# DLRM tower: the last group's squares added on VectorE, group 2's transposed features copied in three parts from another bank, feature transposes ahead of the embedding

## What is computed

```python
e = stack([tbl_f[ids[:, f]] for f in range(26)])               # 512 x 26 x 64
x = layer_norm(dense @ Wd.T)                                   # 512 x 128
y = layer_norm(e @ Ws.T)                                       # 512 x 26 x 128
y = layer_norm(y mixed over the 26 fields by Wsi)              # 32 projections per channel
T = concat([x, y.T])                                           # 33 x 128 per sample
Z = T @ T.T; Zflat = lower triangle of Z                       # 528 pairs
z = layer_norm(Zflat @ Wl.T)[:, :384]                          # over 512 features
h = relu(concat([z, dense]) @ W_top1 + b_top1)                 # 512
h = relu(h @ W_top2 + b_top2)                                  # 256
out = h @ W_top3
```

## Time and profile before

| | |
|---|---|
| median of 3 runs | 171.63 us (170.33 to 172.66) |
| the profiled execution | 171.68 us |
| its span, first to last instruction | 169.9 us |
| instructions in it | 3523 |
| busy, share of the span | PE 149.0 us (88%), DVE 124.9 (74%), POOL 100.6 (59%), ACT 83.7 (49%) |
| mean granted TensorE clock | 0.97 of full speed |

### The profile page before, as it was taken

One profiled execution on the slowest core, in us unless ns is written; L12 is line 12 of the kernel. 1 busy time (PEld: TensorE's weight loads), 2 busy tenths in 40 slices (PEclk: granted clock), 3 DMA queues, 4 the chain that ended last, 5 costly groups with the idle time before them and its releaser, 6 DMA issues.

```text
span 169.9 us, 3523 instructions
## 1 busy us (share of the span) xinstructions
PE 149.0 (88%) x1382; PEld 107.1 (63%) x1382; DVE 124.9 (74%) x256; ACT 83.7 (49%) x224; POOL 100.6 (59%) x109
## 2 busy tenths in 40 slices
PE   0489878997968797999999899999998999899995
PEld 0324466945545665646978475678876665689994
DVE  6595838978808796777589998486998987993153
ACT  3012243329677829686646465653538363653250
POOL 1777777777777777777777777777777400030000
PEclk9999999579997899999999999999999999999999
DMA  4913651625121111111111111121111100000000
GB/s 104 335 24 58 207 137 41 203 42 147 23 35 25 32 24 23 35 23 34 24 23 34 24 23 35 23 32 28 23 33 27 23 0 4 0 0 4 4 0 0
DMA packets 5728, 8.14 MB, mean 48 GB/s; under 512 B 2357, under 2 KB 3279, under 8 KB 5712
## 3 DMA queue, kind: packets, MB, share of 16 engines
q0 software_dynamic: 3328, 3.41, 10.9%
q1 hardware_dynamic: 1664, 3.65, 6.8%
q10 hardware_dynamic: 720, 0.85, 1.5%
HBM read 7.91 MB, written 0.00 MB: 47 GB/s over the span
## 4 chain that ended last, share of the span: by engine, by line
PE 50%; DVE 17%; ACT 12%; POOL 11%; issue 7%; DMA 1%; DVEq 0%
POOL G L332 11%; PE ps_tail L1116 8%; PE ps_y L1067 6%; PE ps_tail L1132 5%; PE ps_z L1074 5%; PE ps_gq L1042 5%; PE ps_ut L1054 4%; DVE V L794 4%; DVE V L778 3%; PE ps_z L1162 3%; PE ps_tail L1026 3%; ACT sq L438 2%; DVE var L750 2%; DVE var L785 2%; ACT gt L424 2%
## 5 line engine op out<-in xcount | busy, mean ns | idle before, releaser
L332 POOL DMA_INDIRECT G<-in_table_dram,idx x104 | 98.4, 947 | 34.9 <-issue 31.1
L1054 PE MATMUL ps_ut<-S,G 128*128 128x192 f32 (+4 forms) x128 | 21.8, 316 | 0.4 <-DVE G L764 0.4
L778 DVE TENSOR_TENSOR V<-ps_y,bias_y 128x512 f32<-128x512 f32 x32 | 20.5, 682 | 1.5 <-PE ps_y L1067 1.4
L1074 PEld LDWEIGHTS ps_z<-V 128*64 128x64 f32 x448 | 15.1, 142 | 10.0 <-DVE V L794 6.2
L1054 PEld LDWEIGHTS ps_ut<-S,G 128*128 128x128 f32 x128 | 20.1, 199 | 2.0 <-DVE G L764 1.8
L1042 PE MATMUL ps_gq<-gram,gt 128*128 128x128 f32 x104 | 15.9, 293 | 6.0 <-ACT gt L424 5.7
L785 DVE TENSOR_REDUCE var<-sq 128x32 f32<-128x1024 f32 x14 | 17.1, 1220 | 5.4 <-ACT sq L438 5.4
L438 ACT ACTIVATE sq<-V 128x1024 f32<-128x1024 f32 x14 | 14.9, 1061 | 11.1 <-DVE V L778 11.1
L1067 PE MATMUL ps_y<-ut,wcg 64*128 64x512 f32 x64 | 19.5, 686 | 0.5 <-issue 0.4
L1042 PEld LDWEIGHTS ps_gq<-gram,gt 128*128 128x128 f32 x104 | 13.5, 199 | 7.5 <-ACT gt L424 6.5
L1074 PE MATMUL ps_z<-V 128*64 128x67 f32 x448 | 17.1, 231 | 0.2
(11 more groups left out here) (179 smaller groups left out, 235.3 us busy)
## 6 DMA issues: line engine op xcount, KB each, us to landing
G<-in_table_dram,idx POOLq DMA_INDIRECT x104, 2.4
w1z<-in_w_z_dram SPq DMA_DIRECT2D x1, 768.0 KB, 4.3
wl<-in_wl_blocks_dram SPq DMA_DIRECT2D x1, 768.0 KB, 5.8
dns<-in_dense_t_dram ACTq DMA_DIRECT2D x1, 512.0 KB, 4.7
w1d<-in_w_d_dram SPq DMA_DIRECT2D x1, 512.0 KB, 5.1
wl<-in_wl_blocks_dram SPq DMA_DIRECT2D x1, 512.0 KB, 3.7
w2s<-in_w_dram SPq DMA_DIRECT2D x1, 512.0 KB, 3.6
wrow<-in_wsi_rows_dram SPq DMA_DIRECT2D x1, 208.0 KB
```

What stands on the lines that cost most here:

```text
L332: pool.indirect_dma_start(G[:, n // NC, j, g, :], None, table, bass.IndirectOffsetOnAxis(ap=idx[:, k:k + 1], axis=0)).then_inc(gathered[n ...
L778: dve.tensor_tensor(chunk_v(n)[:, g * CB // 2:(g + 1) * CB // 2, :, :], ps_y[:, g, :].rearrange("p (b l q) -> p b l q", l=2, q=NPROJ), bia ...
L1054: mm = pe.matmul(ps_ut[:, chunk % 2, col:col + width], G[:, gp, j, :, :].rearrange("p g d -> p (g d)"), S[:, j, :, :].rearrange("p s q -> ...
L1074: mm = pe.matmul(z_bank(n)[64 * ct:64 * ct + 64, w, s * SLOTS:(s + 1) * SLOTS], V[:, v, 3:SLOTS], V[:, v, :], start=True, stop=True)
```

## The change

It has four parts. In slots 7 and 11, TensorE's `transpose_features` stands ahead of `embed`, and ScalarE's `f_scale` ahead of `ut_copy`. For group 2, the transposes go to the bank `ps_gq`, ScalarE copies them to `zn` in three pieces of 128 columns, and `layer1` waits for one piece at a time in its first block. In the last group, VectorE adds the squares of blocks 3, 0 and 1 into `f_acc` in two additions, and TensorE sums `f_acc` and the square of block 2 by two matmuls instead of four. And GpSimd multiplies the second half of the dense part by `sd3`, in place of VectorE.

```diff
--- before.py
+++ after.py
@@ -160,6 +160,7 @@
         f_scaled = sb("f_scaled", [P, LLIVE, P])
         f_sq = sb("f_sq", [P, LC, GRAN])
         f_sum = sb("f_sum", [P, 1])
+        f_acc = sb("f_acc", [P, GRAN])
         sd3 = sb("sd3", [P, GRAN])
         r3 = sb("r3", [P, GRAN])
         dense_sd = sb("dense_sd", [P, OC1, GRAN])
@@ -220,7 +221,7 @@
             sem("h1_ps"), sem("h1_pre_ready"), sem("h1_ready"), sem("h2_ps"), sem("h2_ready"))
         own_sq_ready, b2_ready, h1_last_ps, h1_scaled, h1_last_pre, h1_last_ready, h2_last_ps, h2_last_ready = [sem(n) for n in (
             "own_sq_ready", "b2_ready", "h1_last_ps", "h1_scaled", "h1_last_pre", "h1_last_ready", "h2_last_ps", "h2_last_ready")]
-        floor2_ready = sem("floor2_ready")
+        floor2_ready, f_acc_ready, dense_sd_pool = sem("floor2_ready"), sem("f_acc_ready"), sem("dense_sd_pool")
         yo_ps, yo_ready, stored = sem("yo_ps"), sem("yo_ready"), sem("stored")
 
         dense_banks = (ps_tail[:, :], ps_z[:, 1, :])
@@ -338,6 +339,11 @@
             pool.tensor_tensor(chunk_v(n), chunk_v(n), r2_pool[:, :].rearrange("p (b l) -> p b l", l=2).unsqueeze(3).broadcast_to([P, CB, 2, NPROJ]),
                                ALU.mult).then_inc(v_pool_ready, 1)
 
+            gp = NG - 1
+            pool.wait_ge(sd3_ready, gp + 1)
+            pool.tensor_tensor(dense_sd[:, half_ocs(1), :], h1_dense[:, half_ocs(1), gp * GRAN:(gp + 1) * GRAN],
+                               sd3[:, :].unsqueeze(1).broadcast_to([P, OC1 // 2, GRAN]), ALU.mult).then_inc(dense_sd_pool, 1)
+
         @block.scalar
         def _(act):
             act.dma_start(wc[:, :], ws_t).then_inc(ld_wc, 16)
@@ -476,7 +482,12 @@
 
             def zn_copy(gp):
                 act.wait_ge(ft_ps, gp + 1)
-                act.copy(zn[:, :, :], tail[:, 0:LLIVE, :]).then_inc(zn_ready, 1)
+                act.copy(zn[:, :, :], tail[:, 0:LLIVE, :]).then_inc(zn_ready, LLIVE)
+
+            def zn_copy_parts(gp):
+                act.wait_ge(ft_ps, gp + 1)
+                for k in range(LLIVE):
+                    act.copy(zn[:, k, :], ps_gq[:, k * P:(k + 1) * P]).then_inc(zn_ready, 1)
 
             def relu1(gp):
                 act.wait_ge(h1_pre_ready, gp + 1)
@@ -539,13 +550,13 @@
                 gt_copy(n)
                 if c < 3:
                     deviation2(n - 2)
+                if c == 3 and gp > 0:
+                    f_scale(gp - 1)
                 ut_copy(n - 1)
                 if c == 0 and gp > 1:
                     relu1(gp - 2)
                 if c == 2 and gp > 0:
                     z_copy(gp - 1)
-                if c == 3 and gp > 0:
-                    f_scale(gp - 1)
                 if n == 3:
                     prepare_means(0)
                 if n == 4:
@@ -608,7 +619,7 @@
             deviation3(gp - 1)
             ut_copy(n)
             f_scale(gp - 1)
-            zn_copy(gp - 1)
+            zn_copy_parts(gp - 1)
             deviation2(n - 1)
             last_square2(n, 0)
             last_square2(n, 1)
@@ -860,16 +871,23 @@
             def last_f_copy(gp):
 
                 for lc in range(LLIVE):
+                    if lc == LLIVE - 1:
+
+                        dve.wait_ge(f_sq_ready, gp + 2)
+                        dve.tensor_tensor(f_acc[:, :], f_sq[:, LLIVE, :], f_sq[:, 0, :], ALU.add).then_inc(f_acc_ready, 1)
                     dve.wait_ge(f_ps, gp + 2 + lc)
                     dve.tensor_copy(f_sb[:, lc, :], last_f_banks[lc]).then_inc(f_ready, 1)
+                dve.wait_ge(f_sq_ready, gp + 3)
+                dve.wait_ge(f_acc_ready, 1)
+                dve.tensor_tensor(f_acc[:, :], f_acc[:, :], f_sq[:, 1, :], ALU.add).then_inc(f_acc_ready, 1)
 
             def last_add_dense(gp):
 
                 dve.wait_ge(sd3_ready, gp + 1)
+                dve.tensor_tensor(dense_sd[:, half_ocs(0), :], h1_dense[:, half_ocs(0), gp * GRAN:(gp + 1) * GRAN],
+                                  sd3[:, :].unsqueeze(1).broadcast_to([P, OC1 // 2, GRAN]), ALU.mult).then_inc(h1_scaled, 1)
                 for h in range(2):
-                    dve.tensor_tensor(dense_sd[:, half_ocs(h), :], h1_dense[:, half_ocs(h), gp * GRAN:(gp + 1) * GRAN],
-                                      sd3[:, :].unsqueeze(1).broadcast_to([P, OC1 // 2, GRAN]), ALU.mult).then_inc(h1_scaled, 1)
-                    dve.wait_ge(h1_scaled, h + 1)
+                    dve.wait_ge((h1_scaled, dense_sd_pool)[h], 1)
                     dve.wait_ge(h1_last_ps, 1 + h)
                     dve.tensor_tensor(h1_pre_last[:, half_ocs(h), :], last_h1_ps[:, h, :, :], dense_sd[:, half_ocs(h), :],
                                       ALU.add).then_inc(h1_last_pre, 1)
@@ -1126,9 +1144,10 @@
 
             def layer1(gp, ocs=range(OC1)):
                 pe.wait_ge(w1_ready, 1)
-                pe.wait_ge(zn_ready, gp + 1)
                 for oc in ocs:
                     for k in range(LLIVE):
+                        if oc == 0:
+                            pe.wait_ge(zn_ready, gp * LLIVE + k + 1)
                         mm = pe.matmul(tail[:, oc, :], w1z[:, k, oc * P:(oc + 1) * P], zn[:, k, :],
                                        start=(k == 0), stop=(k == LLIVE - 1))
                 if OC1 - 1 in ocs:
@@ -1184,13 +1203,12 @@
                                    start=(k == 0), stop=(k == KB - 1))
                 mm.then_inc(f_ps, 1)
 
-            def last_sum_squares(gp, lc):
-
-                place = LAST_ORDER.index(lc)
-                pe.wait_ge(f_sq_ready, gp + 1 + place)
-                mm = pe.matmul(last_ss_ps, ones[:, :], f_sq[:, lc, :], start=(place == 0), stop=(place == LC - 1))
-                if place == LC - 1:
-                    mm.then_inc(ss_ps, 1)
+            def last_sum_squares(gp):
+
+                pe.wait_ge(f_acc_ready, 2)
+                pe.matmul(last_ss_ps, ones[:, :], f_acc[:, :], start=True, stop=False)
+                pe.wait_ge(f_sq_ready, gp + LC)
+                pe.matmul(last_ss_ps, ones[:, :], f_sq[:, LLIVE - 1, :], start=False, stop=True).then_inc(ss_ps, 1)
 
             def last_layer1(gp, ocs):
                 for oc in ocs:
@@ -1231,9 +1249,9 @@
                 gram_rows(n)
                 if c == 2 and gp > 0:
                     spread_pairs(gp - 1)
-                embed(n - 1)
                 if c == 3 and gp > 0:
                     transpose_features(gp - 1)
+                embed(n - 1)
                 pair_products(n - 2)
                 if c == 0 and gp > 1:
                     layer2(gp - 2)
@@ -1287,7 +1305,11 @@
             project_fields(n)
             pair_products(n - 2)
             embed(n)
-            transpose_features(gp - 1)
+            pe.wait_ge(f_ready, gp)
+            pe.wait_ge(q_used, NCHUNK)
+            for k in range(LLIVE):
+                mm = pe.transpose(ps_gq[:, k * P:(k + 1) * P], f_scaled[:, k, :], eye[:, :])
+            mm.then_inc(ft_ps, 1)
             layer1(gp - 1)
             pair_products(n - 1)
             last_pair_products(n, 0)
@@ -1296,15 +1318,10 @@
             spread_pairs(gp)
             layer2(gp - 1, range(1, OC2))
 
-            last_project_pairs(gp, 3)
-            last_project_pairs(gp, 0)
-            last_sum_squares(gp, 3)
-            last_project_pairs(gp, 1)
-            last_sum_squares(gp, 0)
-            last_project_pairs(gp, 2)
-            last_sum_squares(gp, 1)
+            for lc in LAST_ORDER:
+                last_project_pairs(gp, lc)
             last_layer1(gp, range(0, 1))
-            last_sum_squares(gp, 2)
+            last_sum_squares(gp)
             last_layer1(gp, range(1, OC1))
             layer3(gp - 1)
             last_layer2(gp)
```

## The result

The changed kernel takes 173.69 us (median of 6 runs, 172.47 to 174.47) against 171.68 us for the kernel before (6 runs, 170.33 to 172.66) in the same measurement. The ratio is 1.0111 with a 95% interval of 1.0071 to 1.0150: slower by 1.9 us by the ratio and by 2.0 between the medians, and outside the range, which was predicted to end at 172.4.

What follows compares the result with a forecast made beforehand. TensorE was taken to bound the kernel, with 50% of the chain that ended last; the four parts' terms, 0 + 0 - 0.5 + 0, took 171.68 to 171.2 us, range 170.1 to 172.4.

Steps and rivals of the forecast that it cites:

- rival of a mutual lock (B): Last group's dense product: VectorE's and GpSimd's halves exclude each other, the first ReLU comes late, up to 172.3; chance 0.07.
- signs that the prediction listed: Two sums of squares; PE idle about 0.25 in group 2; slots 7, 11 unchanged; GpSimd's dense product 0.5 to 0.7.
- Rival C: Last group's copy, addition and square outlast layer 1's first quarter, or moved embedding's cover fails: 0.1 to 0.3 lost; chance 0.12.
- The cover of VectorE's additions: Slots 7 and 11: embedding halves ready 0.09 and 0.20 before VectorE's additions want them; otherwise late by at most 0.48.
- rival A: Group 2: pair products do not wait for V, so the earlier layer 1 gains 0.27 more, 170.9; chance 0.08.

## Why the prediction was wrong

The forecast of 171.2 us, half a microsecond faster, missed one part, which is worth more than the three others together. For these three its sum, 0.5, is close to the 0.6 of the traces, but partly by luck: the sums of squares were put 0.17 too high, and a gain of 0.3 from the order of the transposes was excluded. Only the copy in three parts came out as reasoned.

**The dense half on GpSimd: the step that failed.** It was put at 0, because the product is wanted at 164.54 and had 1.7 us of cover. That looked at who waits for the product, and stopped there. What follows it in GpSimd's own queue is the end of the program, where the drain ends 8.6 us after GpSimd's last instruction. It ended 10.8 us early before (158.8 against 169.7). The new last instruction ends at 162.89 + 0.97 in the run with it alone, 13.6 later than the product of V (150.23): that uses up the 10.8 and 2.8 more. The prediction had asked for other steps what stands behind them in the queue, and not for this one; the row was in the trace of before, under the line at which the block ends. The rival of a mutual lock (B) had the right part and the right sign, by luck: its mechanism was another, and VectorE's product took 0.42 at its usual place. None of the signs that the prediction listed looked at the program's end.

**GpSimd's product itself** was put at 0.48 by columns, with 1.92 as the bound, and expected to take 0.5 to 0.7; it took 0.97. VectorE's half started at 160.84 and ended at 161.26, GpSimd's started at 160.88. If it stood until VectorE's had ended, 0.59 is left for the product, which is near the estimate. The Trainium skill ("SBUF — State Buffer", section "Who interferes with whom") says that the second of two such instructions blocks until the first ends, and the 0.97 agrees with it in size; no run here has the product on GpSimd without VectorE's beside it, so it is not shown.

**The sums of squares** were put at 0.5, bounds 0.35 to 0.54. They gave 0.33 in the traces, alone and in the changed kernel. The term was mis-sized at the first block of layer 1: 0.87 instead of 0.67. With t for the end of the last projection, the copy ends at t + 0.33, and the third pair was reckoned to need it at t + 0.44. It needs it earlier. The chain sets each row behind the modelled end of the row before, but a matmul starts before that end, and its weight load, which stands behind the same wait, 0.11 before the matmul. In the changed kernel t is 159.08, and the block's weight loads start at 158.81, 158.92, 159.03 and 159.15. The fifth, the third pair's, was due at 159.26, so at t + 0.18. The copy, and this one load by itself:

```profile
159.12 0.29 DVE L879 COPY f_sb<-ps_z 128x128 f32<-128x128 f32 x1 [0.63 <-PE ps_z L1202]
...
159.47 0.19 PEld L1218 LDWEIGHTS ps_ut<-f_sb,w1z 128*128 128x128 f32 x1
```

The load starts 0.21 late, just behind the end of the copy at 159.41. In the kernel before, a sum of 0.22 stood ahead of the block, the same load was due at t + 0.40 (161.61), the copy was there at 161.54, and nothing waited. Rival C had the size of this (0.1 to 0.3 of the gain) but not the place: neither the addition nor the last square was waited for.

**The transposes ahead of the embedding** were put at 0, since only the sum of TensorE's work counts. The sum was not the same: one weight load that was exposed now runs beside other matmuls. 0.15 in each slot, a gain, where the prediction excluded one. The bound on that side was closed by a reason ("TensorE has no idle time there to give back") that looked at whether TensorE was busy, and not at what its time was made of; a weight load with nothing beside it counts as busy too. The cover of VectorE's additions was wrong too: they wait 0.23 for the embedding in slot 7 of the changed kernel, where 0.09 to spare was reckoned. That they are not in the chain there held.

**The copy in three parts** was put at 0, with an idle TensorE before the pair products and V as the cause. The run of it alone gives 1.0000 (0.9974 to 1.0026) and shows that wait, the pair products starting 4.15 behind group 2's transposes, where it was 4.16 before. The interval alone would not exclude rival A's 0.27 us (0.16%); these rows do.

The sum, with the terms that the traces give: -0.33 - 0.3 + 0 + 2.8 = +2.2, against 2.0 between the medians and 1.9 by the ratio. The terms may be added, because the root that releases GpSimd's product stands behind the sums of squares and comes earlier by the first two.

## What to carry to other kernels

An instruction that is moved to an idle engine late in a program has two deadlines: the one of its consumer, and the one of the engine's own end. Look at the row of the line at which the block ends, for each engine, and at how long its drain lasts; for GpSimd it was 8.6 us from the end of its last instruction, so by these figures no instruction of this kernel may end there in the last 8.6 us. And where the span grows while the last arithmetic row comes earlier, the answer stands behind that row.

## What the runs showed of the hardware

GpSimd's drain at the end of the program ended 8.6 us after its last instruction had ended, whatever that was: a product of 1024 columns, one of 256, a memset of one column, the issue of a gather (8.57 to 8.59 in fourteen traces). At the program's start it lasted 187 ns behind memsets of one column. On the other engines the same instruction at the end lasted 589 ns (ScalarE), 630 (TensorE), 291 (VectorE) and 7 (SP). The Trainium skill ("VectorE: DVE Perf Modes", section "The DRAIN you can't avoid") speaks of drains of about 12 ns on all five engines, from what the runtime puts ahead of a kernel and behind it. At this program's start four engines are near that (7 to 10 ns in the changed kernel) and GpSimd is not; at its end only SP is, and GpSimd's drain, 8.7 to 11.4 us, is over 700 times as long. The measurement decides; whether these rows are the drains that the page means, none of them says. What the 8.6 us are spent on stays open: no run here varied anything but the last instruction.

The first matmul behind the embedding's 512-column matmuls had its weight load exposed in slots 7 and 11 of each kernel read (its load and the matmul both start at 111.32 in the kernel before, at 111.99 with the new order), and a group of full weights behind weights of one column took 0.2 us longer (0.86 for 0.67, 0.64 for 0.45). A weight load that waits for a copy was due 0.11 us before its matmul, and 0.26 before the place that the chain's lengths gave (t + 0.18 against t + 0.44).
